# Four layers on one core: where batch 1's maxima, its row parts and two late maxima stand in the second attention's written order

## The reference

```python
x = _layernorm(x + _L0_attn_ref(x, ...))   # grouped-query attention, 16 heads of 16, not causal
x = _layernorm(x + _L0_ffn_ref(x, ...))    # a shared expert and the best one of 8 experts
x = _layernorm(x + _L1_attn_ref(x, ...))   # the part that the change touches:
    qkv = x @ W_qkv.T + b_qkv              # 16 heads of 16 features
    scores = jnp.einsum('bnqd,bnkd->bnqk', q, k) * scale
    scores = jnp.where(causal, -jnp.inf, scores)
    attn = jax.nn.softmax(scores, axis=-1)
    out = jnp.einsum('bnqk,bnkd->bnqd', attn, v) @ W_out.T + b_out
x = _layernorm(x + _L1_ffn_ref(x, ...))    # 256 -> 1024 -> 256, relu, 4-bit weights and a low-rank product
return x
```

## Time and profile before

| | |
|---|---|
| median of 3 runs | 808.87 us (807.51 to 809.41) |
| the profiled execution | 804.52 us, span 802.8 us |
| TensorE matmul busy | 755.4 us, 94% of the span |
| VectorE, ScalarE, GpSimd busy | 446.9, 398.7, 126.8 us |
| mean granted TensorE clock | 0.990 |

### The profile page before, as it was taken

One profiled execution on the slowest core, in us unless ns is written; L12 is line 12 of the kernel. 1 busy time (PEld: TensorE's weight loads), 2 busy tenths in 40 slices (PEclk: granted clock), 3 DMA queues, 4 the chain that ended last, 5 costly groups with the idle time before them and its releaser, 6 DMA issues. The chain is left out here.

```text
span 802.8 us, 12486 instructions
## 1 busy us (share of the span) xinstructions
PE 755.4 (94%) x4393; PEld 446.3 (56%) x4394; DVE 446.9 (56%) x1194; ACT 398.7 (50%) x593; POOL 126.8 (16%) x135
## 2 busy tenths in 40 slices
PE   8899999999999999999999897989989998999996
PEld 4323434444434589999977554435445644653685
DVE  4663744565354722222228798939685667563464
ACT  3499775786595154454525325465333453146230
POOL 0000000000000131111563372223101110022100
PEclk9999999999999999999999999989999999999999
DMA  7668116105106262111123882005600280000000
GB/s 230 182 204 280 43 35 191 51 27 155 42 27 218 72 183 76 46 52 46 39 70 109 242 260 81 2 2 153 189 1 3 79 234 6 26 1 27 0 27 27
DMA packets 53822, 75.03 MB, mean 93 GB/s; under 512 B 7926, under 2 KB 45082, under 8 KB 53386
## 3 DMA queue, kind: packets, MB, share of 16 engines
q1 hardware_dynamic: 51900, 69.26, 28.0%
q0 software_dynamic: 1872, 5.11, 2.4%
HBM read 46.57 MB, written 27.66 MB: 92 GB/s over the span
## 5 line engine op out<-in xcount | busy, mean ns | idle before, releaser
L676 PE MATMUL ps<-arena 128*128 128x256 f32 (+3 forms) x1084 | 315.8, 439 | 5.6 <-DVE arena L1217 1.4
L676 PEld LDWEIGHTS ps<-arena 128*128 128x128 f32 x1084 | 196.1, 190 | 87.9 <-issue 55.4
L1003 ACT ACTIVATE arena<-ps 128x1024 f32<-128x1024 f32 x128 | 124.1, 1029 | 25.6 <-PE ps L744 25.3
L1118 ACT ACTIVATE arena<-ps 128x1024 f32<-128x1024 f32 (+3 forms) x128 | 82.9, 702 | 99.0 <-PE ps L928 98.8
L1496 DVE TENSOR_REDUCE arena<-ps 128x1 f32<-128x384 f32 (+3 forms) x176 | 100.5, 634 | 26.0 <-PE ps L906 25.3
L806 PE MATMUL ps<-arena 128*128 128x128 f32 x736 | 89.4, 275 | 0.6 <-DVE arena L1228 0.6
L806 PEld LDWEIGHTS ps<-arena 128*128 128x128 f32 x736 | 87.4, 192 | 2.4 <-issue 1.3
L1622 POOL TENSOR_SCALAR_AFFINE_SELECT arena<-arena 128x512 f32<-128x512 f32 x64 | 42.5, 664 | 218.4 <-ACT arena L1118 218.4
L904 PE MATMUL ps<-arena 96*128 96x128 bf16 (+3 forms) x256 | 62.3, 306 | 12.0 <-DVE arena L1496 7.3
L744 PE MATMUL ps<-arena 96*128 96x512 bf16 x256 | 69.7, 382 | 4.2 <-ACT arena L1003 2.7
L758 PE MATMUL ps<-arena 128*32 128x512 f32 x512 | 68.8, 604 | 0.3 <-ACT arena L1010 0.3
(11 more groups left out here) (160 smaller groups left out, 755.3 us busy)
## 6 DMA issues: line engine op xcount, KB each, us to landing
arena<-stacks_dram SPq DMA_DIRECT2D x32, 384.0 KB, 6.3
arena<-in_gate_up_proj SPq DMA_DIRECT2D x8, 1024.0 KB, 9.3
stacks_dram<-arena SPq DMA_DIRECT2D x16, 384.0 KB, 3.7
arena<-in_down_proj SPq DMA_DIRECT2D x8, 512.0 KB, 9.0
stacks_dram<-arena SPq DMA_DIRECT2D x16, 256.0 KB, 4.0
q_stacks_dram<-arena SPq DMA_DIRECT2D x8, 384.0 KB, 3.3
arena<-q_stacks_dram SPq DMA_DIRECT2D x8, 384.0 KB, 4.8
arena<-q_stacks_dram SPq DMA_DIRECT2D x4, 768.0 KB, 5.8
```

What stands on the lines that cost most here:

```text
L676: last = nc.tensor.matmul(dst[0:rows, lo:hi], a, w, start=(n == 0), stop=(n == len(pairs) - 1))
L1003: nc.scalar.activation(probs[:, 2 * p:2 * p + 2, :], ps[:, 2 * p:2 * p + 2, :], ACT.Exp)\
L1118: nc.scalar.activation(cprobs[:, i % 2, 2 * p:2 * p + 2, P * kt:S], ps[:, 2 * p:2 * p + 2, P * kt:S], ACT.Exp).then_inc(exp_done[p], 1)
```

## The change

Three changes of order in the strings, and the bookkeeping that lets a batch's maxima be spread over two strings (`m` counts for each batch). No instruction is added or removed, and every size is kept.

1. Four of batch 1's maxima stand at the end of `C_START`, ahead of `cE` of batch 2 and of batch 0's S(0). In `C_FIRST` the rest follow: the same numbers of maxima in slots 0 to 9, three in slot 10, none in slot 11.
2. `cm` of batch 1 stands in slot 11, ahead of `cF2` in slot 12. It stood behind `cF2`. `cM` stays in slot 13.
3. In `C_SECOND` and `C_THIRD` slot 11 has two maxima, not four, and slot 12 has three, `cD0` and five, not two, `cD0` and four.

The rotation of the three banks is unchanged in `C_START` and `C_FIRST`. In part 3 `cD0` comes one step earlier in it, so that its bank is that of the maximum with index 29 and no longer that of index 30.

```diff
@@ C_START, C_FIRST, C_SECOND (C_THIRD is changed in the same places)
-cm0 +cV0 Wd3 >cL0 >cL1 cM0 Wdl3 +cV1 >cE0"""
+cm0 +cV0 Wd3 >cL0 >cL1 cM0 Wdl3 +cV1 +m +m +m +m >cE0"""
 C_FIRST = """+m +m +m | +m +m +m +m | +m +m +m +m | +m +m +m +m | .cF0 +m +m +m | +m +m +m +m | +m +m +m +m
-| +m +m +m +m | .cF1 +m +m +m | +m +m +m +m | +m +m +m +m | +m +m +m | .cF2 +cm0 | +cM0 | | |"""
+| +m +m +m +m | .cF1 +m +m +m | +m +m +m +m | +m +m +m | +cm0 | .cF2 | +cM0 | | |"""
...
-| +m +m -cH5 +m +m +m =cO0 >cL0 >cL1 +m +m | =cO1 >cE0 -cH6 -cH7 +m +m +m +m | .cF2 +m +m -cD0 +m +m +m +m
+| +m +m -cH5 +m +m +m =cO0 >cL0 >cL1 +m +m | =cO1 >cE0 -cH6 -cH7 +m +m | .cF2 +m +m +m -cD0 +m +m +m +m +m
 | +m +m +m +m +m +m +m +cm0 -cD1 +cM0 | -cD2 | |"""
...
@@ expand, attention_order, c_order
             if to < B:
-                steps.append(("max", to, m[0]))
-            m[0] += 1
+                steps.append(("max", to, m[to]))
+            m[to] += 1
...
-        m = [0]
...
+    m = [0] * (B + 1)
+    return (expand(C_START, 0, m) + attention_order([C_FIRST, C_SECOND, C_THIRD, C_LAST], "catt", m)
+            + expand(C_END, B, []))
```

More of the change, by code:

```diff
@@ L83 @@
 m m m m m m +cQ1 +cK1 m m m m m m +cQ2 +cK2 m m m m m m m +cQ3 +cK3 m m m Wdl0 m m m m Wdl1 m m m Wdl2 m m m m m m m m m m m
-cm0 +cV0 Wd3 >cL0 >cL1 cM0 Wdl3 +cV1 >cE0"""
+cm0 +cV0 Wd3 >cL0 >cL1 cM0 Wdl3 +cV1 +m +m +m +m >cE0"""
 C_FIRST = """+m +m +m | +m +m +m +m | +m +m +m +m | +m +m +m +m | .cF0 +m +m +m | +m +m +m +m | +m +m +m +m
-| +m +m +m +m | .cF1 +m +m +m | +m +m +m +m | +m +m +m +m | +m +m +m | .cF2 +cm0 | +cM0 | | |"""
-C_SECOND = """-cF3 +cX0 +cX1 | +cQ0 -cP0 | +cK0 -cP1 +cQ1 | =cD3 +cK1 +cQ2 | .cF0 +cV0 +cK2 +cV1 | +cQ3 -cN0 -cN1
-| -cH0 +cK3 +m +m +m | -cH1 +m +m +m -cH2 +m +m +m | .cF1 -cH3 +m +m +m +m +m | +m +m +m -cH4 +m +m +m
-| +m +m -cH5 +m +m +m =cO0 >cL0 >cL1 +m +m | =cO1 >cE0 -cH6 -cH7 +m +m +m +m | .cF2 +m +m -cD0 +m +m +m +m
[L90 to L94, removed]
+| +m +m +m +m | .cF1 +m +m +m | +m +m +m +m | +m +m +m | +cm0 | .cF2 | +cM0 | | |"""
+C_SECOND = """-cF3 +cX0 +cX1 | +cQ0 -cP0 | +cK0 -cP1 +cQ1 | =cD3 +cK1 +cQ2 | .cF0 +cV0 +cK2 +cV1 | +cQ3 -cN0 -cN1 | -cH0 +cK3 +m +m +m | -cH1 +m +m +m -cH2 +m +m +m | .cF1 -cH3 +m +m +m +m +m | +m +m +m -cH4 +m +m +m | +m +m -cH5 +m +m +m =cO0 >cL0 >cL1 +m +m | =cO1 >cE0 -cH6 -cH7 +m +m | .cF2 +m +m +m -cD0 +m +m +m +m +m | +m +m +m +m +m +m +m +cm0 -cD1 +cM0 | -cD2 | |"""
+C_THIRD = """-cF3 +cX0 +cX1 | +cQ0 -cP0 | +cK0 -cP1 +cQ1 | =cD3 +cK1 +cQ2 | .cF0 +cV0 +cK2 +cV1 | +cQ3 -cN0 -cN1 >cL0 >cL1 >cE0 | -cH0 +cK3 +m +m +m | -cH1 +m +m +m -cH2 +m +m +m | .cF1 -cH3 +m +m +m +m +m | +m +m +m -cH4 +m +m +m | +m +m -cH5 +m +m +m =cO0 +m +m | =cO1 -cH6 -cH7 +m +m | .cF2 +m +m +m -cD0 +m +m +m +m +m | +m +m +m +m +m +m +m +cm0 -cD1 +cM0 | -cD2 | |"""
 C_LAST = """-cF3 | -cP0 | -cP1 | =cD3 | .cF0 -cN0 -cN1 =cO0 | -cH0 -cH1 =cO1 | -cH2 | -cH3 | .cF1 -cH4 | -cH5 | |
@@ L116, in expand, with attention_order @@
     return steps
-def attention_order(fills, name):
+def attention_order(fills, name, m):
     steps = []
@@ L134, in attention_order @@
             steps.append((name + "P", b, i))
-        assert m[0] in (0, len(MAXES)), m
+    assert m[0:B] in ([0] * B, [len(MAXES)] * B), m
     return steps
 def a_order():
-    return (expand(A_START, 0, [0]) + attention_order([A_FIRST, A_SECOND, A_THIRD, A_LAST], "att")
-            + expand(A_END, B, [0]))
+    return (expand(A_START, 0, []) + attention_order([A_FIRST, A_SECOND, A_THIRD, A_LAST], "att", [0] * B)
+            + expand(A_END, B, []))
 def c_order():
-    return (expand(C_START, 0, [0]) + attention_order([C_FIRST, C_SECOND, C_THIRD, C_LAST], "catt")
-            + expand(C_END, B, [0]))
+    m = [0] * (B + 1)
+    return (expand(C_START, 0, m) + attention_order([C_FIRST, C_SECOND, C_THIRD, C_LAST], "catt", m)
+            + expand(C_END, B, []))
 def post_ln_layers(nc, ins, out):
```

## The result

The changed kernel takes 810.88 us (median of 8 runs, 808.70 to 811.77), the kernel before 806.62 us (8 runs, 804.20 to 809.41). The ratio is 1.0053, 95% interval 1.0037 to 1.0069: 4.3 us slower. The profiled execution took 811.12 us, span 809.4 us, 6.6 us more than that of before (804.52 us).

The account below looks back on a forecast made before the run. TensorE's own order (94% busy) was taken to set the time, broken by short waits for banks VectorE has not read out. Terms 1.3 + 0 + 2.4 = +3.7 us on the 808.87 us median gave 812.6 us, range 807.9 to 816.0.

Parts of the forecast that it names:

- Part 1, start: Batch 0's start: four maxima make S(0) 2.5 us late; the 1.20 us wait moves from max 3 to max 7.
- Part 1, end: Batch 0's slots 11 to 15: with less cover, P(12) waits for the mask, 1.3 us later than before.
- Part 2: `cm` ahead of `cF2`: `cM` and its DMAs stay put, so the 1.77 us wait stays; value 0, at best 0.3 us.
- Part 3, the order: Slots 11 and 12, batches 1 and 2: `cD0` 0.6 us late behind `cF2`, fifth maximum 0.6 us; 1.2 us each, +2.4 us.
- Part 3, the term that was missing: At `cD0` in batches 1 and 2: a new wait of 1.5 us or so, with no charge for half clock.
- my own list of signs: Profile checks: wrong if `cD0` starts without a wait, the DMA wait is gone, or a half-clock stretch appears or vanishes.
- the sum: Whole kernel: 1.3 + 0 + 2.4 = +3.7 us, with the norm losing the same to GpSimd's masks; otherwise +2.8 us.
- A: Slots 11 and 12: P(11) and S(13) fill the 1.17 to 1.55 us waits; up to -3 us, about 806.5 us; chance 0.12.
- B: Part 1 costs TensorE nothing and part 3's fifth maximum behind `cD0` hides: +1.2 us, 810.1 us; chance 0.18.
- C: Batch 0's start and slots 11 to 15: second half-clock stretch, 816 us, chance 0.1; its absence, 809.2 us, chance 0.05.
- D: Whole kernel: the change does nothing because other semaphores set the pace; 808.9 us; chance 0.05.

Follow-up runs that it names:

- e2_part1: Kernel before with four maxima ahead of batch 0's S(0) and slot 11 empty, `cm` still behind `cF2`; 806.60 us against 805.80, ratio 1.0006.
- e3: Kernel before with only `cm` of batch 1 moved ahead of `cF2`; 807.10 us against 805.80, ratio 1.0012.
- e4_clock: Changed kernel with two unread filler matmuls in the wait ahead of `cD0` in batches 1 and 2; 807.73 us, ratio 1.0020 against before's 805.80.
- e8: Kernel before with two maxima ahead of batch 0's S(0) and one in slot 11; 809.88 us against 806.27, ratio 1.0037.
- e5: Like e1_part3, but on VectorE `cF2` stands behind max 29 and 30, not ahead of max 29; 804.56 us against before's 806.27, ratio 0.9977.
- e1_part3: Kernel before with only the new order of `C_SECOND` and `C_THIRD`; 811.13 us against 805.80, ratio 1.0057.
- e6: Kernel before with unread filler matmuls: two ahead of batch 1's S(0), two and one ahead of max 30 of batches 2 and 3; 803.65 us against 806.27.
- e7: Like e5, plus two filler matmuls ahead of batch 1's S(0); 802.90 us against before's 806.27, ratio 0.9965.
- e9: Whole change with `cF2` behind max 29 and 30 and two fillers ahead of batch 1's S(0); 803.01 us against before's 805.49, ratio 0.9959.
- e10: The kernel of e7 run again, on the same chip as e9; 802.97 us against before's 805.49, ratio 0.9956.

## Why the prediction was right, and where it was not

- **Direction and size.** Forecast +3.7 us and a median of 812.6 us; measured +4.3 us and 810.9 us, both within what was forecast. The base had moved: with more runs the kernel before has a median of 806.6 us, not 808.9. That the two changes lie so near to each other is in part luck, as said below.
- **Part 1, start: right.** The changed profile has `cM0` 0.16 us later than before (482.46 against 482.30), so 0.16 us comes off its times here. S(0) of batch 0 at 488.67, forecast 488.7. Max 7 at 495.44, forecast 495.35, though its wait of 1.2 us is not in the profile: half clock stretched P(0) from 1.06 to 1.73 us and took the wait's place. In e2_part1, without half clock, it is there with 1.23 us.
- **Part 1, end: right, a little oversized.** S(12) at 522.25 (forecast 522.7), S(12) to P(12) 3.57 us (3.45, and 3.92 before) with the mask as releaser, and the wait of 1.77 us for the DMAs unchanged. Net +0.97 us against my 1.3: the carried schedule put S(12) 0.45 us too late and the mask 0.12 us too early.
- **Part 2: right for the whole change**, at zero. Alone it costs 0.59 us (e3), which is the bound that I should have named for the case that VectorE is still busy. The steps that I had for the whole change (the parts ready earlier, `cM` and the DMAs as before) are what the rows show.
- **Part 3, the order: right.** e4_clock measures it without the clock: 1.22 and 1.24 us where I had worked out 1.2. `cD0` is 0.68 us late against S(12) (forecast 0.6) and P(12) follows its start by 5.86 us (5.9), 0.55 us more than before.
- **Part 3, the term that was missing.** I forecast the wait ahead of `cD0` and charged nothing for what it does to the clock, although showed the clock fall behind a wait of 1.77 us, as long as the new one. It adds 1.7 us in each batch, 3.4 us in all, as much as the whole order does (0.97 + 1.22 + 1.24 = 3.4 us). By my own list of signs (I am wrong if a stretch at half clock appears), the sum had this wrong.
- **Why the median came out near all the same.** The change between the profiled executions is 6.6 us, not 3.7. But the profiled execution of before lies 2.1 us below its median, and that of the changed kernel (811.12) within 0.3 us of its own. Before pays part of the 3.4 us too, in some executions: its 1.55 us wait was followed by half clock in two of the four profiles with that order in batch 1 (e2 and e8, not before and e3), and the profiled execution of before was one without. The runs point the same way: of the 35 of before that were measured beside e5, the three fastest (803.7 to 804.1 us) have a mean granted clock of 0.990, the three slowest (809.6 to 810.0 us) 0.982. So a missing term of 3.4 us and a fast profile largely cancelled in the median; that was luck. I put the change on the median because the rows didn't show what sets the profiled execution apart, and not because I knew this.
- **Rivals.** A falls: P(11) and S(13) do fill the wait, and the kernel is slower. With `cF2` moved as well (e5), a gain is there, but small: 0.3 us in each stretch, 0.23% in the median. B falls: part 1 costs 1.0 us and part 3 is not halved. C named the right thing in the wrong place: it looked for a second fall in batch 0, where one came and cost nothing (49.31 against 49.32 us in e2_part1), and the two that cost 3.4 us lie ahead of `cD0` in batches 1 and 2. Its chance of 0.1 was too low: a fall came at this wait in all four places that have it unfilled (two batches in the changed kernel, two in e1_part3). D falls.

## What to carry to other kernels

When a step moves, look at what it stands behind on every engine: here TensorE's order improved and VectorE's order took it back, and moving one step of VectorE by two places was worth 3 us a batch. A wait of some 1.5 us or more on TensorE may have to be charged twice, for itself and for the matmuls behind it at half clock; below are the cases here. Matmuls that nobody reads, in a wait that can't be removed, gave 1.7 us in each place in e4 and 2.3 us in e6. Executions of one kernel differ by such falls, so one profile on each side is not a measure of a change of a few us, and a table by stretches, with the half-clock time beside each, separates what the medians hide.

## What the runs showed of the hardware

- At the 1.77 us wait ahead of batch 1's S(0) the clock fell in all 8 profiles without fillers there (from 0.5 us before the wait's end to 2.6 us after it), and in none of the 4 with them (e6, e7, e9, e10). At the 1.74 us wait ahead of `cD0` it fell in 4 of 4 cases (from 0.4 us before its end to 0.5 us after), and in neither of the 2 that e4 filled. Behind the 1.54 to 1.55 us wait it fell in 2 of 4, behind batch 1's 0.94 us wait followed by one of 0.24 us in 1 of 4 (e10, not e5, e7, e9), and behind the 1.17 us wait in none of 4 (batch 2 in before, e2, e3, e8). Each fall ahead of the kernel's tail lasted 3.4 or 6.8 us in all profiles.
- The length of a wait alone does not tell. Behind the 1.20 to 1.23 us wait in batch 0's start (492.8 to 496.1 us) the clock fell in 2 of 6 profiles (e3, e6; not before, e2, e4, e7), within 1.6 us. Behind a wait of 1.73 us ahead of `cM0` in e2_part1 (483.20) none came for 50 us, and behind waits of 1.39 to 1.43 us in batch 1 (558 to 564 us) none in six profiles (the changed kernel, e2, e4, e5, e6, e8). What decides between them stays open.
- A fall costs 1.7 us of 3.4 where TensorE is the limit (`cD0` 5.38 against 3.67 us), and nothing where TensorE would have waited for VectorE: cM0 to S(0) of batch 1 takes 48.34 to 48.35 us in e1_part3, e5 and e10 with a fall at 489 to 493, and 48.34 in before and e7 without one; in the changed kernel and e2_part1 it is 49.31 and 49.32.
- The moments of the falls moved between two executions of one program, on two chips (e7 and e10 are the same kernel: 454 and 21 us in one, 22, 39, 489 and 595 us in the other). This agrees with what the prediction cited of the Trainium skill (TensorE: Matmul & The Clock Gate, "Part 1: The HAM clock gate"), that the watch runs freely.
- The norm on VectorE was held by GpSimd's two masks before and after. Before, one step of 0.16 us took 0.52 us and one 0.62 us, each until a mask ended. In the changed kernel L1171 at 491.66 took 0.53 us, to 492.19, when the mask of 491.54 + 0.64 us ended, and one of L1177's four steps, under the mask of 493.25, took 0.81 us where the others took 0.40 to 0.41. The norm took 4.61 us before and 4.56 us after, so the move changed nothing there, as the sum had it.
